# A new order of loads and of every engine's steps in a four-batch attention and graph kernel

## The reference

```python
# layer 0: low-rank update. lora_A is the context, lora_B and the router are weights
w = softmax(x @ router_W.T + router_b)               # 8 experts
a_sum = einsum('bsh,arh->bsr', x, lora_A)            # 64 columns
x = nan_to_num(x + 0.5 * einsum('bsn,bsnh->bsh', w, einsum('bsr,nhr->bsnh', a_sum, lora_B)))
# layer 1: cross attention on the context, 32 heads of 16, mask, output weights, layer norm
x = layernorm(x + attention(x @ Wq, ctx @ Wk, ctx @ Wv) @ Wo) * ln_g + ln_b
# layers 2 and 3, the same: 8 nearest neighbours of each of the 512 points, 4 blocks
idx = top_k(-distance(ctx), 8)
for i in range(4):
    p = leaky_relu(x)
    x = (w_center[i] @ p + sum_k(w_neighbor[i] @ p[idx_k])) / 9 + x
```

## Time and profile before

| what | value |
|---|---|
| median of 3 runs | 377.6 us (377.03 to 379.24) |
| span of the profiled execution, first to last instruction | 378.0 us |
| busy: TensorE, VectorE, ScalarE, GpSimd | 367.6, 272.0, 177.0, 129.0 us |
| mean granted TensorE clock | 0.995 |

### The profile page before, as it was taken

The page is one execution under the profiler, slowest core; times in us unless marked ns, Lnnn a source line. Parts: engine busy times, 40 slices in busy tenths (PEclk is TensorE's granted clock), DMA queues, the critical chain, the costliest instruction groups (busy, mean ns, idle before and its releaser), DMA issues.

```text
span 378.0 us, 6569 instructions
## 1 busy us (share of the span) xinstructions
PE 367.6 (97%) x2396; PEld 311.0 (82%) x2396; DVE 272.0 (72%) x427; ACT 177.0 (47%) x308; POOL 129.0 (34%) x125
## 2 busy tenths in 40 slices
PE   7799999999999999999999999999999999999996
PEld 4475897787887877877798889898989889898895
DVE  4926799997899898678858994467686475566524
ACT  2238348758888675374425262234224233424311
POOL 5058416110401405005162345444537224344320
PEclk9999999999999999999999999999999999999999
DMA  6995116207108405400000000000000000000023
GB/s 201 317 348 159 24 55 155 78 9 178 34 20 232 105 0 116 102 0 3 0 3 2 0 0 2 0 2 1 2 0 2 0 2 0 3 0 2 0 85 139
DMA packets 25056, 22.47 MB, mean 59 GB/s; under 512 B 9537, under 2 KB 20546, under 8 KB 25026
## 3 DMA queue, kind: packets, MB, share of 16 engines
q1 hardware_dynamic: 24352, 22.04, 20.9%
q10 hardware_dynamic: 674, 0.02, 0.1%
HBM read 12.35 MB, written 3.15 MB: 41 GB/s over the span
## 4 chain that ended last, share of the span: by engine, by line
PE 85%; DVE 4%; ACT 4%; DMA 3%; issue 2%; SPq 1%; DVEq 0%; ACTq 0%
PE slot L564 82%; DMA wk<-in_WkT 3%; ACT k_blk_hi L943 2%; PE slot L684 1%; PE slot L693 1%; SPq L448 1%; PE slot L725 1%; ACT probT L976 1%; DVE p_full L1321 1%; DVE points L1331 1%; ACT adj L874 1%; DVE inv_full L1267 0%; ACT L976 0%; DVE stats L1282 0%; DVE shift L1255 0%
## 5 line engine op out<-in xcount | busy, mean ns | idle before, releaser
L1065 POOL TENSOR_TENSOR p_lo<-p_full,p_hi 128x512 fp32r<-128x512 f32 x64 | 86.0, 1362 | 157.1 <-ACT p_hi L1016 157.0
L1026 ACT ACTIVATE u_hi<-slot 128x512 fp32r<-128x512 f32 x64 | 36.2, 593 | 69.3 <-PE slot L564 69.0
L1326 DVE TENSOR_TENSOR u_lo<-slot,u_hi 128x512 fp32r<-128x512 f32 x64 | 42.4, 684 | 31.5 <-ACT u_hi L1026 31.5
L1016 ACT ACTIVATE p_hi<-p_full 128x512 fp32r<-128x512 f32 x64 | 39.0, 627 | 55.3 <-DVE p_full L1321 55.3
L564 PE MATMUL slot<-adj,u_hi 128*128 128x512 f32 x256 | 64.8, 392 | 0.1
L564 PE MATMUL slot<-fs_hi,p_hi 128*128 128x256 f32 x256 | 64.8, 286 | 0.0
L1331 DVE SCALAR_TENSOR_TENSOR points<-slot,points 128x512 f32<-128x512 f32 x64 | 42.7, 684 | 30.4 <-PE slot L564 30.4
L564 PE MATMUL slot<-adj,u_lo 128*128 128x512 f32 x256 | 64.1, 391 | 0.0
L564 PE MATMUL slot<-fs_lo,p_hi 128*128 128x256 f32 x256 | 64.1, 283 | 0.0
L1321 DVE SCALAR_TENSOR_TENSOR p_full<-points 128x512 f32<-128x512 f32 x64 | 54.3, 863 | 8.9 <-POOL p_lo L1065 6.3
L564 PEld LDWEIGHTS slot<-adj,u_lo 128*128 128x128 f32 x256 | 47.5, 188 | 10.1 <-issue 0.4
(11 more groups left out here) (144 smaller groups left out, 569.1 us busy)
## 6 DMA issues: line engine op xcount, KB each, us to landing
q_stack<-q_hi SPq DMA_DIRECT2D x32, 128.0 KB, 2.5
x_in<-in_xT SPq DMA_DIRECT2D x8, 256.0 KB, 4.2
q_stack<-q_lo SPq DMA_DIRECT2D x16, 128.0 KB, 2.4
out_points<-points SPq DMA_DIRECT2D x8, 256.0 KB, 2.0
loraB_raw<-in_lora_BT SPq DMA_DIRECT2D x1, 1024.0 KB, 8.0
wk<-in_WkT SPq DMA_DIRECT2D x1, 1024.0 KB, 11.4
wq_raw<-in_WqT SPq DMA_DIRECT2D x1, 1024.0 KB, 10.5
wv<-in_WvT SPq DMA_DIRECT2D x1, 1024.0 KB, 11.4
```

The lines of the kernel that those rows point to most:

```text
L1016: act.activation(p_hi[b][:, (i % 2) * H:(i % 2 + 1) * H], p_full[:, p_buf[b, i]], ACT.Copy)\
L1026: act.activation(half_of(u_hi[:, u], i % 2), bank("wa", b, i // 2, i % 2), ACT.Copy)\
L1065: pool.tensor_tensor(lo[:, cut], full[:, cut], hi[:, cut].bitcast(F32), ALU.subtract)\
L1326: dve.tensor_tensor(half_of(u_lo[:, u], i % 2), bank("wa", b, i // 2, i % 2), half_of(u_hi[:, u], i % 2).bitcast(F32), ALU.subtract).then_ ...
```

## The change

LOADS: the coordinates of batch 1 (`xyz1`, 2 x 128 KB) go ahead of the low-rank weights (`loraB`, 1 MB), and the keys' weights (`wk`, 1 MB) go behind the rows of batch 1 (`x1`, 2 x 256 KB). All five step strings are replaced: the same steps in another order, with other PSUM banks and buffers. No step is added or removed, and no instruction's shape changes. Before `keys` TensorE now also runs `dist1_0`, `lora1`, `mixed0` and `router1`; `values` stands behind `ua0`, `dist1_1`, `adjT0`, `ub0` and `uc0`.

```diff
-LOADS = "xyz0 ctxT x0 loraB wk xyz1 x1 small wq wv wo"
+LOADS = "xyz0 ctxT x0 xyz1 loraB x1 wk small wq wv wo"
...
 PE_STEPS = """
-mb0:0 dist0_0:7 dist0_1:5 lora0:6 dist0_2:2 dist0_3:4 router0:0 keys:6,7 lora1:2 mixed0:0,1 router1:2 values:4,5
-mixed1:2,0 dist1_0:7 adjT0:4,5 ua0:3,6 ub0 uc0 dist1_1:4 dist1_2:5 ua1:1,2 qa0:7,3 qb0 dist1_3:6 ub1 sc0_0:4,5 qc0
-uc1 sc0_1:0,1 lora2:6 adjT1:2,3 router2:0 dist2_0:1 sc0_2:4,5 sc0_3:6,7 qa1:3,2 dist2_1:7 qb1 dist2_2:4 shift0:5
-dist2_3:1 lora3:6 mixed2:0,3 router3:5 sc1_0:6,7 qc1 ua2:0,4 w0_0:2,3 sc1_1:6,7 ub2 sc1_2:2,3 w0_1:6,7 uc2 w0_2:2,3
-w0_3:6,7 at0_0:0,1,5 at0_1 at0_2 at0_3 sc1_3:6,7 qa2:3,2 qb2 shift1:0 mixed3:6,7 norm0:4,5 qc2 sc2_0:0,1 rows0:5,4
-oa0 sc2_1:0,1 ob0 w1_0:2,3 oc0 sc2_2:6,7 w1_1:0,1 ua3:5,2 sc2_3:6,7 ub3 uc3 w1_2:6,7 shift2:5 at1_0:0,1,3 at1_1
-w1_3:4,5 at1_2 at1_3 rows1:7,4 qa3:2,6 qb3 norm1:0,1 qc3 wa0_0:2,3,0 wb0_0 sc3_0:0,1 wc0_0 wd0_0 oa1 sc3_1:0,1
-sc3_2:2,3 ob1 w2_0:0,1 oc1 w2_1:2,3 sc3_3:0,1 ga0_0:7,6 gb0_0 w2_2:2,3 at2_0:0,1,5 at2_1 gc0_0 gd0_0 w2_3:2,3
-shift3:7 at2_2 at2_3 rows2:2,7 wa1_0:4,6,1 wb1_0 wc1_0 wd1_0 norm2:0,1 wa0_1:5,3,0 wb0_1 wc0_1 oa2 wd0_1 ob2 oc2
-ga1_0:6,0 gb1_0 w3_0:4,5 gc1_0 gd1_0 w3_1:4,5 ga0_1:1,2 gb0_1 gc0_1 w3_2:6,7 at3_0:4,5,3 at3_1 dist3_0:0 w3_3:6,7
...
-gc3_7 gd3_7 ga1_7:3,7 gb1_7 gc1_7 gd1_7
+mb0:4 dist0_2:7 dist0_1:1 lora0:6 router0:0 dist0_0:6 dist0_3:5 dist1_0:4 lora1:3 mixed0:7,2 router1:3 keys:0,1
+ua0:6,3 dist1_1:7 adjT0:0,1 ub0 uc0 values:0,1 mixed1:7,6 dist1_2:2 qa0:3,4 dist1_3:1 qb0 lora2:5 qc0 router2:1
+sc0_0:2,3 ua1:6,0 sc0_2:2,3 mixed2:5,7 ub1 uc1 sc0_1:4,5 sc0_3:2,3 ua2:1,6 ub2 uc2 shift0:0 adjT1:4,5 qa1:2,3 qb1
+dist2_2:6 w0_0:4,5 sc1_0:0,1 qc1 sc1_2:6,7 w0_1:4,5 lora3:2 sc1_1:0,1 dist2_0:3 sc1_3:6,7 w0_2:4,5 at0_0:0,1,2 at0_1
+w0_3:6,7 router3:5 dist2_1:4 at0_2 at0_3 qa2:7,6 mixed3:0,5 shift1:1 qb2 norm0:2,3 qc2 dist2_3:7 sc2_2:0,1 ua3:2,3
+ub3 sc2_0:6,7 uc3 w1_0:4,5 w1_1:6,7 sc2_1:0,1 rows0:3,2 sc2_3:4,5 oa0 w1_2:4,5 at1_0:0,1,6 at1_1 ob0 w1_3:4,5 oc0
+at1_2 at1_3 qa3:5,7 shift2:4 rows1:1,0 norm1:2,3 qb3 qc3 oa1 sc3_1:4,5 sc3_0:2,3 w2_0:6,7 ob1 w2_1:4,5 sc3_2:6,7 oc1
+at2_0:2,3,6 w2_2:4,5 at2_1 w2_3:0,1 sc3_3:4,5 at2_2 at2_3 wa1_0:0,7,1 wa0_0:4,5,0 wb0_0 norm2:2,3 wc0_0 wd0_0
+shift3:6 wb1_0 wc1_0 wd1_0 ga0_0:3,2 ga1_0:5,1 gb0_0 gc0_0 gd0_0 gb1_0 w3_0:6,7 gc1_0 rows2:3,0 gd1_0 oa2 w3_1:4,5
+ob2 at3_0:6,7,1 at3_1 w3_2:4,5 w3_3:2,3 oc2 at3_2 at3_3 wa0_1:2,3,1 wb0_1 wa1_1:4,5,0 norm3:6,7 wb1_1 rows3:0,6
+wc1_1 wd1_1 wc0_1 oa3 wd0_1 ob3 oc3 ga0_1:1,7 gb0_1 gc0_1 gd0_1 adjT2:2,3 dist3_2:1 ga1_1:7,4 gb1_1 gc1_1 gd1_1
+wa0_2:5,1,1 wb0_2 wc0_2 dist3_0:7 wd0_2 dist3_1:3 wa1_2:2,4,0 wb1_2 dist3_3:6 wc1_2 wd1_2 ga0_2:3,5 ga1_2:1,0 gb0_2
...
+gb3_7 gc3_7 ga0_7:6,1 gd3_7 gb0_7 gc0_7 gd0_7
 """
 ACT_STEPS = """
-sq0 low0 rE0 lbh wqh low1 mh0_0 rE1 mh0_1 kh kb0 sq1 woh mh1_0 adjC0 xh0_0 mh1_1 xh0_1 sq2 qh0_0 xb0_0 qf0_0 qh0_1
-xb0_1 qf0_1 xh1_0 low2 adjC1 xh1_1 rE2 kb1 qh1_0 sh0 qf1_0 xb1_1 low3 mh2_0 mh2_1 vb0 qh1_1 qf1_1 rE3 xb1_0 ex0_0
-ex0_1 ex0_2 ex0_3 xh2_0 xh2_1 kb2 ac0_0 ac0_1 qh2_0 sh1 ah0_0 qh2_1 ah0_1 xb2_0 qf2_0 mh3_1 qf2_1 xb2_1 mh3_0 vb1
-ex1_0 dev0 ex1_1 kb3 sh2 ex1_2 xh3_0 ex1_3 xh3_1 fh ph0_0 ac1_1 ac1_0 vb2 qf3_0 qh3_0 ph0_1 qf3_1 ah1_0 qh3_1 xb3_0
-uh0_0 uh0_1 ah1_1 ex2_0 ex2_1 dev1 sq3 ex2_2 ph1_1 ex2_3 sh3 ph1_0 xb3_1 ph0_3 ph0_2 ac2_1 ac2_0 uh1_1 ah2_0 vb3
...
+sq0 sq1 low0 rE0 lbh low1 mh0_1 mh0_0 rE1 kh wqh adjC0 xh0_0 kb0 xb0_1 woh xh0_1 mh1_1 mh1_0 vb0 qf0_0 low2 qh0_0
+rE2 qh0_1 qf0_1 mh2_0 xb0_0 mh2_1 xh1_0 xb1_0 kb1 sh0 sq2 xh1_1 adjC1 qh1_0 qf1_0 ex0_0 qf1_1 qh1_1 ex0_1 xb2_0 low3
+xb1_1 xh2_0 ex0_2 ex0_3 xh2_1 rE3 ac0_1 ac0_0 kb2 mh3_0 sh1 qf2_0 qh2_0 mh3_1 ah0_0 vb1 ah0_1 qh2_1 xb2_1 qf2_1
+ex1_0 ex1_1 xh3_0 kb3 ex1_2 xh3_1 ex1_3 fh dev0 ac1_0 ac1_1 sh2 vb2 ah1_0 ah1_1 qf3_0 qh3_0 qh3_1 sq3 qf3_1 ex2_0
+ph0_1 ph0_0 ex2_1 dev1 ex2_2 ex2_3 ph1_1 ph1_0 xb3_0 vb3 ac2_1 ac2_0 uh0_0 uh0_1 sh3 ah2_1 uh1_0 uh1_1 ah2_0 ex3_0
...
 """
 DVE_STEPS = """
-mr fa a_ready fm init near0_0 rA0 near0_1 near0_3 near0_2 rB0 rA1 mk ml0_0 rB1 kl vr ml0_1 near1_0 ml1_0 raw0_0
-nan0_0 raw0_1 xl0_0 nan0_1 ml1_1 xl0_1 near1_1 near1_2 near1_3 raw1_0 mx0_0 nan1_0 raw1_1 mx0_1 xl1_0 nan1_1 rA2
-mx0_3 xl1_1 mx0_2 near2_0 rB2 near2_1 sl0 near2_2 ml2_0 mx1_0 ml2_1 rA3 near2_3 rB3 mx1_1 raw2_0 mx1_2 nan2_0 raw2_1
-nan2_1 xl2_0 xl2_1 mx1_3 rc0 sl1 dv0_0 dv0_1 al0_0 al0_1 mx2_0 ml3_1 mx2_1 ml3_0 st0_0 ce0_0 st0_1 mx2_2 ce0_1 ln0
-mx2_3 raw3_0 nan3_0 sl2 raw3_1 nan3_1 xl3_0 lk0_0:0 xl3_1 rc1 fl lk0_1:2 dv1_1 dv1_0 al1_0 mx3_0 ul0_0 ul0_1 al1_1
-mx3_1 mx3_2 st1_0 ce1_0 st1_1 mx3_3 ce1_1 ln1 lk1_1:1 lk1_0:0 pt0_0 lk0_2:3 pt0_1 lk0_3:2 sl3 rc2 dv2_0 dv2_1 al2_0
...
+mr fa a_ready fm rA0 near0_2 rB0 near0_1 near0_3 ml0_0 rA1 rB1 ml0_1 near0_0 kl near1_1 raw0_0 nan0_0 raw0_1 near1_0
+init xl0_0 nan0_1 vr xl0_1 near1_3 ml1_0 near1_2 ml1_1 rA2 mx0_0 rB2 mx0_2 ml2_0 raw1_0 nan1_0 mx0_1 ml2_1 raw1_1
+xl1_0 mx0_3 nan1_1 sl0 raw2_1 xl1_1 raw2_0 mk near2_2 mx1_0 nan2_0 mx1_2 mx1_1 mx1_3 nan2_1 xl2_0 rA3 near2_0 xl2_1
+rB3 rc0 sl1 dv0_1 ml3_0 dv0_0 near2_1 mx2_2 ml3_1 near2_3 al0_0 al0_1 mx2_0 raw3_0 raw3_1 nan3_0 mx2_3 mx2_1 nan3_1
+xl3_0 st0_0 xl3_1 ce0_0 st0_1 ce0_1 rc1 ln0 sl2 dv1_0 dv1_1 al1_0 al1_1 lk0_0:2 lk0_1:3 fl mx3_1 mx3_0 st1_0 mx3_2
+st1_1 ce1_1 ce1_0 ln1 lk1_1:1 lk1_0:2 mx3_3 rc2 dv2_1 ul0_0 dv2_0 sl3 ul0_1 ul1_1 ul1_0 al2_0 pt0_0 pt0_1 al2_1
+lk0_3:2 pt1_0 lk1_2:3 pt1_1 lk0_2:0 lk1_3:3 st2_0 ce2_0 st2_1 ce2_1 rc3 dv3_0 al3_0 dv3_1 al3_1 ln2 ul1_3 ul1_2
...
 """
 POOL_STEPS = """
-zb wql lbl zk wol ql0_0 ql0_1 zr ql1_0 ql1_1 ql2_0 ql2_1 diag0 diag1 pl0_0 pl0_1 ql3_0 ql3_1 pl1_1 pl1_0 pl0_2 pl0_3
...
+lbl zr zk zb wql ql0_0 wol ql0_1 ql1_0 ql1_1 ql2_1 ql2_0 diag0 ql3_0 ql3_1 pl0_0 pl0_1 pl1_1 pl1_0 diag1 pl0_3 pl1_2
...
 """
 SP_STEPS = """
-kst ld_xyz2 ks0 ld_x2 qsh0 qs0 ld_x3 sd0 qsh1 qs1 ks1 sd1 ld_fs qsh2 qs2 sd2 ks2 ld_xyz3 qsh3 sd3 ks3 qs3
+kst ld_x2 qsh0 ld_xyz2 ks0 qs0 sd0 ld_x3 qsh1 qs1 ks1 sd1 ld_fs ld_xyz3 qsh2 ks2 sd2 qs2 ks3 qsh3 sd3 qs3
 """
```

More of the change, by code:

```diff
@@ L57 @@
-ga1_0:6,0 gb1_0 w3_0:4,5 gc1_0 gd1_0 w3_1:4,5 ga0_1:1,2 gb0_1 gc0_1 w3_2:6,7 at3_0:4,5,3 at3_1 dist3_0:0 w3_3:6,7
-gd0_1 at3_2 at3_3 wa1_1:1,6,1 wb1_1 wc1_1 adjT2:4,5 dist3_1:7 wd1_1 wa0_2:3,2,0 wb0_2 wc0_2 norm3:0,1 wd0_2 ga1_1:7,6
-gb1_1 gc1_1 gd1_1 ga0_2:2,0 gb0_2 gc0_2 gd0_2 wa2_0:6,1,1 wa1_2:7,3,0 wb1_2 wb2_0 wc1_2 wd1_2 wc2_0 rows3:0,2 oa3 ob3
-oc3 ga1_2:6,7 gb1_2 gc1_2 gd1_2 wd2_0 wa0_3:0,4,0 wb0_3 wc0_3 wd0_3 ga2_0:7,5 gb2_0 gc2_0 gd2_0 dist3_2:2 dist3_3:3
-wa1_3:6,1,1 wb1_3 wc1_3 ga0_3:5,4 wd1_3 gb0_3 gc0_3 gd0_3 adjT3:2,3 wa3_0:1,7,0 wb3_0 wc3_0 ga1_3:2,5 gb1_3 wd3_0
@@ new lines @@
+ob2 at3_0:6,7,1 at3_1 w3_2:4,5 w3_3:2,3 oc2 at3_2 at3_3 wa0_1:2,3,1 wb0_1 wa1_1:4,5,0 norm3:6,7 wb1_1 rows3:0,6
+wc1_1 wd1_1 wc0_1 oa3 wd0_1 ob3 oc3 ga0_1:1,7 gb0_1 gc0_1 gd0_1 adjT2:2,3 dist3_2:1 ga1_1:7,4 gb1_1 gc1_1 gd1_1
+wa0_2:5,1,1 wb0_2 wc0_2 dist3_0:7 wd0_2 dist3_1:3 wa1_2:2,4,0 wb1_2 dist3_3:6 wc1_2 wd1_2 ga0_2:3,5 ga1_2:1,0 gb0_2
+gc0_2 gd0_2 gb1_2 gc1_2 gd1_2 wa2_0:6,7,1 wb2_0 wc2_0 wd2_0 wa0_3:0,3,0 ga2_0:4,1 gb2_0 gc2_0 adjT3:6,7 wb0_3 wc0_3
+wd0_3 gd2_0 wa3_0:5,4,1 wb3_0 ga0_3:6,1 wa1_3:2,0,0 wc3_0 gb0_3 gc0_3 wd3_0 gd0_3 wb1_3 ga3_0:1,7 gb3_0 gc3_0
@@ new lines @@
+wa2_1:4,5,1 wc1_3 gd3_0 wd1_3 wb2_1 wc2_1 wd2_1 ga1_3:6,1 wa3_1:7,2,1 gb1_3 ga2_1:3,4 gb2_1 gc2_1 gd2_1 wb3_1 wc3_1
+gc1_3 gd1_3 wa0_4:0,4,0 wd3_1 ga3_1:7,6 wb0_4 gb3_1 wc0_4 gc3_1 wd0_4 gd3_1 wa2_2:2,0,1 wb2_2 wc2_2 wd2_2 ga0_4:3,6
+gb0_4 gc0_4 ga2_2:1,4 gd0_4 wa3_2:7,5,0 gb2_2 gc2_2 gd2_2 wb3_2 wa1_4:0,6,1 wc3_2 wd3_2 wb1_4 wc1_4 wd1_4 ga3_2:4,5
+gb3_2 ga1_4:1,2 gc3_2 wa2_3:0,3,0 gd3_2 wb2_3 wc2_3 gb1_4 wd2_3 gc1_4 gd1_4 ga2_3:6,4 gb2_3 wa3_3:7,1,1 wb3_3 gc2_3
+wc3_3 gd2_3 wa1_5:0,5,0 wb1_5 wd3_3 wc1_5 ga3_3:7,2 gb3_3 wd1_5 gc3_3 gd3_3 wa2_4:6,1,1 wb2_4 wc2_4 wd2_4 ga1_5:0,2
@@ new lines @@
+dev3 ph0_4 ph1_4 uh0_4 ph1_5 ph2_0 uh0_5 uh1_4 ph2_1 uh1_5 ph3_0 ph0_6 uh2_0 uh2_1 ph1_7 ph0_7 ph3_1 adjC3 uh0_7
+uh0_6 ph1_6 uh3_0 ph2_3 ph2_2 uh3_1 ph0_8 uh1_6 ph3_2 uh1_7 uh2_2 ph0_9 ph3_3 uh2_3 uh3_2 ph2_5 uh3_3 ph2_4 uh0_8
+ph3_5 uh0_9 ph1_8 uh2_4 ph1_9 uh2_5 ph3_4 uh3_5 uh3_4 uh1_8 ph2_7 ph2_6 ph0_11 uh1_9 ph3_6 uh2_6 ph3_7 uh2_7 ph1_10
+ph1_11 uh3_6 ph0_10 uh3_7 ph2_8 uh1_10 ph2_9 uh1_11 uh2_8 uh2_9 ph3_9 ph3_8 ph2_10 uh3_8 uh3_9 ph2_11 ph1_13 ph1_12
+uh0_10 uh0_11 uh2_10 ph3_10 uh2_11 ph3_11 uh3_10 uh3_11 ph0_12 uh1_12 ph2_12 ph2_13 uh1_13 ph3_12 ph3_13 uh2_12
@@ L89 @@
+uh2_13 ph0_13 uh0_12 uh0_13 uh3_12 ph2_14 ph2_15 uh3_13 ph1_14 uh2_14 uh2_15 ph1_15 ph3_14 uh1_14 ph0_14 uh1_15
+ph3_15 ph0_15 uh3_14 uh3_15 uh0_14 uh0_15
 """
 DVE_STEPS = """
[L91 to L93 removed]
@@ new lines @@
+ul1_7 pt3_1 lk0_9:2 ul2_2 lk3_3:1 ul2_3 pt2_3 pt2_2 pt1_6 ul3_2 pt1_7 lk2_5:3 ul3_3 lk2_4:2 lk1_8:1 ul0_8 lk1_9:3
+pt3_3 pt3_2 lk3_5:0 ul0_9 lk3_4:0 ul2_4 pt0_8 ul2_5 pt0_9 pt2_5 ul3_5 pt2_4 lk2_6:3 lk2_7:1 ul3_4 ul1_8 pt3_4
+lk0_11:2 lk3_6:3 pt3_5 lk3_7:1 ul1_9 pt1_9 pt1_8 ul2_6 lk1_10:2 lk1_11:1 ul2_7 lk0_10:0 pt2_6 pt2_7 lk2_8:2 ul3_6
```

(2 more changed lines are left out.)

54 lines of the change are left out of this document (18 added, 36 removed).

## The result

The kernel with the change takes 388.12 us, the median of four runs from 387.46 to 388.81, against 377.40 us for the kernel before in the same session: a ratio of 1.028, with a 95% interval of 1.025 to 1.031. It is slower by 10.7 us, where I had forecast 3.9 us less. The profiled execution took 388.72 us, with a span of 386.9 us and a mean granted clock of 0.996.

What follows compares the result with a forecast made beforehand. TensorE, busy 97% of the span with 85% of the chain, was taken as the bound. 378.0 - 3.0 (start) - 1.3 (`ex` and `rows2` waits) = 373.7 us, adjusted to 373.3 and rounded up to 373.7; range 371.3 to 377.2.

Steps and rivals of the forecast that it cites:

- The start, -3.0 us: Up to `keys`: the 2.43 us hole and 1.75 us of half clock go, less new gaps; gain 3.0 us.
- the half clock belongs to this execution: Rival at `keys`: the median may lack the half clock, so 1.75 us less is won, 375.4 us; chance 0.10.
- the likeliest case: Whole kernel: gains at the start and behind it give 373.7 us, own range 371.3 to 375.6; chance 0.68.
- The `at` steps and `rows2`, -1.3 us: Behind the start: other steps fill the 0.9 us of `ex` waits, and half of the 0.8 us at `rows2` goes.
- Bounds for everything behind 25 us: -3 to +3: From 25 us on: -3 us if all named waits go, +3 if VectorE's fullness makes as many new ones.
- about 3 us of waits against 5 in the old order: TensorE until 115 us: waits at `w0_3` 0.4, `qa2` 0.6, `mixed3` 1.4 and smaller ones; the kernel before loses about 5.
- the graph stage starts with too few batches: Rival, `wa1_0` to `wa2_0`: only two batches have units; over 4.5 us of VectorE queue gives 379 to 381; chance 0.08.
- The range: Whole kernel: 371.3 to 377.2 us, leaving out the slower case and the ends.

Runs made afterwards that it cites:

- e5_front_only: Kernel before with the new LOADS and only the front of the steps reordered, the old order from `ub0` on: 377.52 us, ratio 1.0001.
- e12_before_two_swaps: Kernel before with `w0_3` moved between `at0_1` and `at0_2`, and `wa1_0` ahead of `rows2`: 377.84 us, ratio 1.000.
- e13: Changed kernel with ScalarE's four `dev` steps as Identity instead of Sqrt, so no table loads around them: 386.05 us, ratio 1.023.
- e15: Changed kernel with Identity instead of Sqrt in `dev` and GpSimd writing zeros for the low part of the leaky relu: 379.09 us, ratio 1.005.
- the zeros: GpSimd writes zeros to the low part of the leaky relu instead of subtracting: 382.27 us on the changed kernel, 376.23 us on the kernel before.
- e9: Kernel before with GpSimd writing zeros to the low part of the leaky relu instead of subtracting: 376.23 us, ratio 0.995.
- e10: Changed kernel with three GpSimd memsets in a row for each `pl` instead of the subtraction, reading nothing: 383.18 us, ratio 1.013.
- e11_two_places: Changed kernel with `ob1` ahead of `w2_0`, `oc1` ahead of `sc3_2`, `st1_1` ahead of `mx3_2`, and `near3_1`, `ul0_4`, `ul0_5` ahead of `ln3`: 385.70 us, ratio 1.020.

## Why the prediction was wrong

**The start, -3.0 us.** Nearly every figure stood: `router0` at 12.17 us (12.1 forecast), `keys` at 17.79 (18.1, between 17.6 and 18.4) for 6.8 us (6.9), `values` at 32.3 (32.8). Between the two profiled executions 3.1 us are won at 40 us. The error is in what it was measured against. The rival "the half clock belongs to this execution" was right, and should have set the sum instead of holding 0.10: the 1.75 us are in some executions of before only, by their mean clocks 17 of 60, and the hole differs too, 2.43 us there and 1.55 in the run without the square root. Against that start 0.8 us or less are left at 40 us, and `e5_front_only` shows none of it at the end. The sum had a second fault at the same place: it took the profiled execution as 0.4 us above the median by setting a span against times. It stands 2.4 us above, so that gains read from it could not be taken off a figure so near the median. (The upper end of the likeliest case, 375.6, doesn't follow from its own terms either: 377.6 - 1.3 - 0 is 376.3.)

**The `at` steps and `rows2`, -1.3 us.** From 140 to 180 us, where `rows2` lies, the new order does lose 0.9 us less. The two waits for `ex` stood at 85.64 and 116.02 us in the old order. They are gone, but the stretch that they lie in, 40 to 120 us, loses 0.8 us more than before. And two of these moves put into the old order bring nothing (`e12_before_two_swaps`), since other waits take the place of those that they fill.

**"Bounds for everything behind 25 us: -3 to +3".** This is the step that failed. Behind 40 us the new order loses 12.0 us more between the two profiled executions, 1.7 of them by its stretch at 1.2 GHz. I followed the strings with the durations of the trace up to 120 us and took the rest as like the old order, so the bound had no row under it for the last two thirds of the kernel. Up to 120 us the steps begin within 1 us of the forecast, but the waits were not those that I had named: `mixed3` and `qa2` stood less than 0.2 us, while `qb0`, `sc1_3` and `w1_1` waited 0.74, 0.76 and 0.42 us. I had counted about 3 us of waits against 5 in the old order; the stretch from 40 to 120 us lost 7.8 us against 7.0. That is small beside what lay behind 120 us, three things.

1. *SyncE's chain.* The diff showed the moved string. 20 transfers at 0.6 us and a landing of 3.6 us are 16 us between `w1_3` and `w2_0`, and the new TensorE string has less between them. About 1.3 us, read from the chain and from the wait that stays when the table loads are taken away (1.08 us in e13, 1.4 in e15); no run takes it away. Not tried: a second queue for these transfers.
2. *Table loads.* I did not follow ScalarE there. Between two `ex` a `dev` takes 0.3 + 2 x 1.28 us. In both orders `dev1` stands between `ex2_1` and `ex2_2`, and the new one even has two loads fewer in all. But the old TensorE string has `ga0_0 gb0_0` and `gc0_0 gd0_0` around `w2_2` and `at2_1`, four steps of a graph unit that need nothing from ScalarE's queue of that moment, and the new one has, behind `oc1`, only `ex`'s own consumers and `sc3_3` in a row. Worth 2.1 to 2.4 us in the new order, 0.4 to 0.6 in the old one. That the four steps are the cover is read from the strings and was not tried by itself.
3. *VectorE's steps beside GpSimd.* My price for `lk` in the chain of a unit was an average over steps alone and beside `pl`; for `ln` I had none. The rival "the graph stage starts with too few batches" had the right stage and sign at 0.08, with about 1 us for each of five pairs, 379 to 381 us. It said that the time decides if VectorE's queue eats more than 4.5 us, and did not see what makes it do so. Like with like the zeros are worth 6.1 us in the new order and 2.0 in the old one; of the 6.1, 4.3 are the stretched steps, the hole at 198 us among them, and 1.8 the time of `pl` itself, which I had not put into the unit's chain.

2 and 3 account for more than half of the difference. At full clock it is 387.5 - 377.3 = 10.2 us. Without 2 and 3 the new order stands at 379.1, and the old one would stand at 374.9 if its two small gains added (377.3 - 0.4 - 2.0, a run that wasn't made). Of the 4.2 us that are left, 1.1 to 1.4 are the wait for the transfers. The rest is open. By the count, e15 loses 3.5 us from 120 to 140 us and 1.8 from 180 to 200 us, where e9, the old order with zeros, loses 0.4 and 0.1; in the second stretch it is several waits of 0.4 us, which I have not taken apart.

**The range.** 371.3 to 377.2 let everything behind 25 us cost 3 us at most. With a bound from the rows, the full stretch of every `lk` (12 us on VectorE) and five table loads of 1.28 us (6.4 us), it would have reached to 373.7 + 18.4 = 392 us.

## What to carry to other kernels

A new order of a kernel that is 97% busy is judged by its whole length: follow each engine's queue to the end, transfers, table loads and shared buffers too, before the gain at the start is counted. Take durations from the condition in which the step will run: the same VectorE instruction took 0.7 us alone and up to 1.8 us beside a reading GpSimd instruction, and what that cost depended on the order around it (2.0 us or 6.1 us for the same 11 to 12 us). A hole in one execution, above all one with half clock, is worth what it costs in the median execution; two or three profiles of the kernel before would have told that. Small differences of medians are read like with like: the share of executions with a stretch at half clock moved them here by up to 0.9 us. And a span of the profile is compared with spans, not with times.

## What the runs showed of the hardware

- GpSimd's subtraction stretches VectorE instructions whose inputs all lie in SBUF, from 0.68 to as much as 1.80 us (`lk`) and from 0.75 to 1.8 us (`ln`); memsets of GpSimd of nearly the same total length (1.26 us, in e10) leave `lk` at 0.70.
- A change of ScalarE's table cost 1.28 us each time, with the instruction right behind it (load at 133.43, `dev` at 134.72).
- The same kernel can keep or lose the full clock at one place: TensorE stood 2.43 us and half clock (1.2 GHz) followed, or it stood 1.55 us and 2.4 GHz stayed. The length of the wait alone doesn't decide it: before `ga0_2` at 198 us TensorE stood 1.82 us in the changed kernel and half clock followed, and 1.81 us in `e13_after_no_sqrt` at full clock throughout. In `e11_two_places` 1.43 us of standing, with two more waits close before it, were followed by a stretch at 1.2 GHz (0.59 on average from 134 to 138 us).
- In the changed kernel SyncE issued each of the 20 stack transfers in 0.45 to 0.7 us, so one queue set a pace of 12 us for them.
